# A graph network's forward pass on one core: sources of the 512-wide layer prepared one step earlier, and first-stage rows stored by another queue

## The chip, the cores and the metric

The kernel runs on one core of a Trainium2 chip. The metric is the device time of the whole program in microseconds. Each core has TensorE (PE), VectorE (DVE), ScalarE (ACT), GpSimd (POOL) and SyncE (SP); each runs its own queue of instructions in order, and they meet at semaphores.

## The reference

A graph of 6250 nodes and 100,000 edges, sorted by destination, with 256 values a node. Two residual blocks follow each other:

```
h = relu(layernorm(x)); x = x + attention_layer(h, edges)      # 8 heads, softmax over incoming edges, two batch norms
h = relu(layernorm(x)); x = x + gin(gin(gin(h)))
gin(h) = ((1 + eps) * h + segment_sum(h[src], dst)) @ w + b     # widths 256 -> 512 -> 512 -> 256, relu between
```

The first table stage of this text computes `layernorm`, `relu`, the three projections and the attention scores of every node. The 512-wide layer of this text is the segment sum over rows of 512 values, with the matrix `w3` (512 to 256) applied behind it.

## The kernel before

The nodes are cut into 50 blocks of 125. Phases follow each other with a barrier of all engines and a clearing of the semaphores between them: preparation of edges and of a block adjacency matrix, the first table stage, attention, dense layers, then three aggregation layers, of which `wide_layer` is the second.

**First table stage.** Two helpers matter. `place(b, j)` gives a block with its parity `s`, its index `i` of that parity, and its slot `t` of four x buffers. `over_steps(engine, stages)` writes an engine's program as steps; in step b it runs each `(stage, lag)` on block b - lag. SyncE loads x (`load_x`, L582), waiting from block 4 on for `norm_ready` of the block that had the buffer before. VectorE takes the moments of block b, normalises block b-1 and finishes block b-3 (`finish`: adds biases to the products, reduces to scores, fills `row[s]`, of which there are two). ScalarE takes square roots and copies the turned block; TensorE turns and projects. GpSimd stores `row[s]` to `table0` (`store_row`, L629), after one store of a spare row for each parity (`first_store`), which makes the count on `row_stored` start at one.

**The 512-wide layer.** For every block, GpSimd gathers the rows of the edges' sources from the table in device memory: a round is 17 indirect DMAs of 128 rows of 512 floats into the single buffer `gathered`, in four parts of 4, 4, 4 and 5 tiles; each part waits until TensorE has used that part of the round before (`quarters_used`). VectorE makes 17 one-hot matrices from the destinations, and TensorE adds one-hot times gathered rows in a PSUM bank (L2297, two instructions for each of the 17 products). Then follow `finish` on VectorE (adds the own row and the bias: L2178, L2181), `turn` and `down` on TensorE (the product with `w3_sb`, L2335), `store`, `keep_upper` on ScalarE and `halve` on VectorE, which split the result into an upper and a lower part for the next layer (L2189, L2191, L2216).

Four of the 50 blocks (43, 45, 47, 49: `tabled`) are not gathered. Their sums are made densely in four PSUM banks of their own: for each source block m, its 125 rows are split in an upper and a lower half (`split_source` on VectorE, L2166 and L2168, into the single buffer `source_cut` and half of `source[r]`), ScalarE casts the adjacency part and the upper half (`cast_source`, L2237 and L2239, then issues the load of source m+2), and TensorE multiplies (`source_sums`, L2317, eight products). `source`, `part` and `source_rows` have two buffers each; `source_used[r]` tells that TensorE is done with one.

This layer's `over_steps(engine, stages, beside, early)` runs the stages of step b and then `beside` for source b + `AHEAD`, with `AHEAD = 8` on all three engines. Sources 0 to `early` - 1 come before everything; then the stages of lag 0 for block 0, then the sources up to 7; step 0 has the source alone. Order on the engines in step b:

```
TensorE  rounds of b, turn of b-1, down of b-2, products of source b+8
ScalarE  copy_turned of b-1, store of b-2, keep_upper of b-5, cast of source b+8
VectorE  one-hots of b, finish of b-1, halve of b-4, split of source b+8
```

VectorE runs about a step in front of the others: it makes the one-hots of b+1 while TensorE multiplies block b.

Of the kernel before, what the change touches and what calls it, by code (L numbers as in the profile page):

```python
# [23 lines left out]
BLOCKS = N // NB  # L24
PAIRS = BLOCKS // 2
# [32 lines left out]
AHEAD = 8  # L58
# [34 lines left out]
def build(nc, x, src, dst, Wq, bq, Wk, bk, Wv, bv, Wo, bo, W1, b1, W2, b2, g1, be1, g2, be2,  # L93
# [12 lines left out]
    with ExitStack() as ctx:  # L106
# [63 lines left out]
        def first_store(engine, stored):  # L170

            n = next(spare_rows)
            engine.dma_start(spare[n:n + 1, :], identity[0:1, :]).then_inc(stored, 16)  # L173

        def block_rows(table, b):
            return table[bass.ds(b * NB, NB), :]
# [362 lines left out]
        with ExitStack() as phase:  # L539
# [37 lines left out]
            @block.sync  # L577
            def _(sp):
                def load_x(k):
                    if not isinstance(k.b, int) or k.b >= 4:  # L580
                        sp.wait_ge(norm_ready[k.s], k.i - 1)
                    sp.dma_start(x_sb[k.t][:, :], block_rows(x, k.b)).then_inc(x_loaded[k.t], 16)  # L582

                over_steps(sp, [(load_x, 0)])

            @block.vector
            def _(dve):
# [30 lines left out]
                    order.restart()  # L618

                over_steps(dve, [(statistics, 0), (normalise, 1), (finish, 3)])  # L620

            @block.gpsimd
            def _(pool):
                for s in range(2):
                    first_store(pool, row_stored[s])

                def store_row(k):
                    wait_apart(pool, row_ready[k.s], k.i + 2, 2)
                    pool.dma_start(block_rows(table0, k.b), row[k.s][:, :]).then_inc(row_stored[k.s], 16)  # L629

                over_steps(pool, [(store_row, 3)])
                for s in range(2):
                    pool.wait_ge(row_stored[s], 16 * (PAIRS + 1))

            @block.scalar
            def _(act):
# [1300 lines left out]
        def wide_layer(n, table, w):  # L1937
            k_tiles = w // P
            with ExitStack() as phase:
# [51 lines left out]
                def total_of(s, i):  # L1991
                    return tabled_ps[i - (PAIRS - TABLED)] if tabled(s, i) else sum_ps[s]

                def over_steps(engine, stages, beside=None, early=0):


                    def step(b, j=0):
                        for stage, lag in stages:
                            if b >= first_step and 0 <= b - lag < BLOCKS:
                                stage((b - lag) % 2, 2 * j + (b - lag) // 2)  # L2000
                        if beside is not None and b < BLOCKS - AHEAD:
                            beside(b % 2, b % 4, j + (b + AHEAD) // 4)

                    first_step = 0
                    if beside is not None:
                        for m in range(early):
                            beside(m % 2, m % 4, m // 4)
                        for stage, lag in stages:
                            if lag == 0:
                                stage(0, 0)  # L2010
                        for m in range(early, AHEAD):
                            beside(m % 2, m % 4, m // 4)
                        first_step = 1
                    for b in range(6):
                        step(b)
                    with engine.Fori(0, (BLOCKS - AHEAD - 10) // 4) as j:
                        for b in range(6, 10):
                            step(b, j)
                    for b in range(BLOCKS - AHEAD - 4, BLOCKS + 6):
                        step(b)  # L2020
# [96 lines left out]
                def _(dve):  # L2117
# [74 lines left out]
                                          upper[s][:, :], ALU.subtract).then_inc(lower_ready[s], 1)  # L2192
                        order.restart()

                    over_steps(dve, [(rounds_of, 0), (finish, 1), (halve, 4)], split_source, 6)

                @block.scalar
                def _(act):
# [55 lines left out]
                    for r in range(2):  # L2254
                        load_source(r, r)
                    load_parts(0)
                    over_steps(act, [(load_weights, 0), (copy_turned, 1), (store, 2), (keep_upper, 5)], cast_source, AHEAD)
                    for s in range(2):
                        act.wait_ge(stored[s], 16 * (PAIRS + 1))

# [108 lines left out]
```

## Time and profile before

| | |
|---|---|
| median of 3 runs | 4454.34 us (4452.92 to 4461.15) |
| the profiled execution: time, span | 4454.23 us, 4452.6 us |
| mean granted TensorE clock | 0.885 of 2.4 GHz |
| busy: PE, POOL, DVE, ACT | 80%, 57%, 48%, 28% of the span |
| first table stage | about 313 to 551 us |
| 512-wide layer | about 2742 to 3869 us |

The profile gives each group of instructions its busy time, its idle time before them, and what ended that idle time. A matmul of this kernel's floats is two instructions. The busy share is a mean over stages with different limits; it says little about either stage here.

### The profile page before, as it was taken

What the parts mean: (1) busy time and instruction counts of PE and PEld (TensorE: products, weight loads), DVE (VectorE), ACT (ScalarE), POOL (GpSimd) and SP (SyncE); (2) the same over time, 40 slices, a digit from 0 to 9 for tenths busy, and PEclk for the clock granted to TensorE, in tenths of its full rate; (3) what the DMA queues carried; (4) which work ended last, traced back from release to release, by engine and by line L of the source; (5) the groups of instructions that cost most, each with busy time, mean ns of one, the idle gap of its engine ahead of it and who ended that gap; (6) DMA issues with size and microseconds to landing.
All of it is one profiled execution on the core that took longest, in us unless ns stands there. A gap on an engine that the chain in (4) does not pass through costs nothing. (4 is left out here: it accounts for less than half of the span.)

```text
span 4452.6 us, 70250 instructions
## 1 busy us (share of the span) xinstructions
PE 3560.6 (80%) x16469; PEld 2364.4 (53%) x16470; DVE 2157.3 (48%) x7818; ACT 1265.9 (28%) x2537; POOL 2558.3 (57%) x2766
## 2 busy tenths in 40 slices
PE   3876557777777778876999997888888988788887
PEld 1223345555555557764777774444444444466665
DVE  6987667777777773362222221323322232233333
ACT  3972122222222222372333332001111011122222
POOL 5001177777777760035666663677776776477776
PEclk9999967787877789957999998999999999888888
DMA  4432144444444430067888885777777777599999
GB/s 141 173 155 59 49 112 111 112 112 112 112 112 112 112 101 1 29 188 211 244 245 245 244 243 166 223 233 232 235 235 231 234 234 227 181 286 294 296 293 268
DMA packets 388059, 801.61 MB, mean 180 GB/s; under 512 B 81225, under 2 KB 147513, under 8 KB 384614
## 3 DMA queue, kind: packets, MB, share of 16 engines
q0 software_dynamic: 244224, 577.30, 45.9%
q10 hardware_dynamic: 86354, 138.42, 9.7%
q1 hardware_dynamic: 57360, 84.55, 5.8%
q8 instruction: 44, 0.72, 0.1%
q14 instruction: 77, 0.62, 0.0%
HBM read 699.79 MB, written 100.24 MB: 180 GB/s over the span
## 5 line engine op out<-in xcount | busy, mean ns | idle before, releaser
L1702 POOL DMA_INDIRECT l_gathered<-table,record x850 | 809.5, 952 | 375.6 <-issue 245.8
L815 POOL DMA_INDIRECT a_gathered<-table,record x850 | 810.1, 953 | 302.9 <-issue 256.9
L2107 POOL DMA_INDIRECT l_gathered<-table,record x782 | 749.7, 959 | 374.2 <-issue 261.8
L2297 PE MATMUL bank<-l_gathered,l_onehot 128*125 128x512 f32 x1564 | 699.1, 605 | 18.7 <-DVE l_onehot L2152 15.6
L1139 PE MATMUL bank<-a_gathered,a_onehot 128*125 128x264 f32 x1700 | 520.3, 466 | 75.8 <-DVE a_gathered L943 75.7
L2297 PEld LDWEIGHTS bank<-l_gathered,l_onehot 128*125 128x125 f32 x1564 | 301.7, 194 | 397.5 <-issue 382.9
L1804 ACT ACTIVATE l_part<-l_packed 128x1000 fp32r<-128x1000 bf16 (+1 forms) x300 | 314.4, 1072 | 543.3 <-PE bank L1880 378.9
L1139 PEld LDWEIGHTS bank<-a_gathered,a_onehot 128*125 128x125 f32 x1700 | 374.5, 229 | 171.9 <-DVE a_gathered L943 50.8
L1880 PE MATMUL bank<-rows_last,l_part 125*125 125x512 f32 x1250 | 328.0, 426 | 25.1 <-ACT l_part L1804 18.0
L1880 PE MATMUL bank<-rows_first,l_part 125*125 125x512 f32 x1250 | 308.7, 406 | 29.7 <-ACT l_part L1804 29.7
L1899 PE MATMUL bank<-l_gathered,l_onehot 128*125 128x512 f32 x850 | 245.6, 437 | 105.6 <-DMA l_gathered<-table,record 105.4
L1880 PEld LDWEIGHTS bank<-rows_last,l_part 125*125 125x125 f32 x1250 | 253.3, 205 | 96.0 <-issue 31.8
L1880 PEld LDWEIGHTS bank<-rows_first,l_part 125*125 125x125 f32 x1250 | 234.4, 188 | 99.4 <-issue 40.4
L2178 DVE SCALAR_TENSOR_TENSOR l_z<-l_own,one_eps,bank 125x512 f32<-125x512 f32 x50 | 37.3, 747 | 506.7 <-PE bank L2305 498.5
L2206 ACT ACTIVATE l_zT<-bank 128x500 f32<-128x500 f32 x50 | 29.4, 587 | 862.3 <-PE bank L2326 862.3
L943 DVE TENSOR_TENSOR a_gathered<-a_gathered,bank 128x1024 f32<-128x1024 f32 x200 | 244.1, 1283 | 31.6 <-ACT bank L1082 31.6
L1899 PEld LDWEIGHTS bank<-l_gathered,l_onehot 128*125 128x125 f32 x850 | 165.9, 200 | 167.1 <-DMA l_gathered<-table,record 124.6
L2317 PE MATMUL bank<-l_source,l_part 125*125 125x512 f32 x400 | 139.3, 508 | 135.1 <-ACT l_source L2239 129.5
L173 POOL DMA_DIRECT2D spare<-identity x6 | 3.1, 537 | 420.8 <-POOLq L161 420.8
L533 PE MATMUL bank<-d_code_hot,d_low_hot 128*128 128x250 bf16 x625 | 205.9, 378 | 22.9 <-DVE d_code_hot L495 5.4
L510 ACT ACTIVATE d_stage<-bank 128x500 bf16<-128x500 f32 (+1 forms) x325 | 220.7, 726 | 9.3 <-PE bank L533 7.0
L1763 DVE SCALAR_TENSOR_TENSOR l_work<-rows_first,one_eps,bank 125x256 f32<-125x256 f32 x50 | 24.0, 481 | 402.7 <-PE bank L1907 402.7
(276 smaller groups left out, 5415.6 us busy)
## 6 DMA issues: line engine op xcount, KB each, us to landing
l_packed<-adjacency ACTq DMA_DIRECT2D x201, 250.0 KB, 5.1
adjacency<-d_stage SPq DMA_DIRECT2D x25, 1562.5 KB, 5.2
l_packed<-adjacency ACTq DMA_DIRECT2D x100, 281.2 KB, 5.9
l_gathered<-table,record POOLq DMA_INDIRECT x1632, 4.8
a_gathered<-table,record POOLq DMA_INDIRECT x850
table<-rows_first POOLq DMA_DIRECT2D x50, 250.0 KB
table<-l_work ACTq DMA_DIRECT2D x50, 250.0 KB
l_source_rows<-table ACTq DMA_DIRECT2D x50, 250.0 KB
```

The source lines that it names most:

```text
L510: act.activation(stage[d % 2][:, :, GD * g0:GD * g1].rearrange("p h (g n) -> p g h n", n=GD), banks[(d * NH + h) % 7][:, 0:(g1 - g0) * COD ...
L533: pe.matmul(banks[n % 7][:, (g - g0) * CODES:(g - g0 + 1) * CODES], low_hot[at % HOT][:, :], code_hot[at % HOT][:, :], start=True, stop=Tr ...
L815: pool.indirect_dma_start(out=gathered0[s][:, j * TW:(j + 1) * TW], out_offset=None, in_=table0, in_offset=bass.IndirectOffsetOnAxis(ap=re ...
L943: dve.tensor_tensor(values[:, j0:j1], values[:, j0:j1], factors[:, j0:j1, :].unsqueeze(3).broadcast_to([P, j1 - j0, HEADS, DH]), ALU.mult) ...
L1139: last = pe.matmul(acc_ps[s][0:NB, 0:TW], onehot[s][:, j, :], rows[:, j, :], start=(j == 0), stop=(j == T - 1), skip_group_check=True)
L1702: pool.indirect_dma_start(out=gathered[g][:, j, :], out_offset=None, in_=table, in_offset=bass.IndirectOffsetOnAxis(ap=record[k.t][:, j, 0 ...
L1804: act.activation(part[r][:, 0:h1 - h0, :].rearrange("p h n -> p (h n)"), packed[r][:, 0:h1 - h0, :].rearrange("p h n -> p (h n)"), ACT.Cop ...
L1880: last = pe.matmul(sum_ps[k.s][0:NB, :], part[r][0:NB, h - h0, :], rows_sb[:, h, :], start=(h == 0), stop=False, skip_group_check=True)
L1899: last = pe.matmul(total, onehot[k.t][:, j, :], gathered[g][:, j, :], start=False, stop=(j == T - 1), skip_group_check=True)
L2107: pool.indirect_dma_start(out=gathered[:, j * w:(j + 1) * w], out_offset=None, in_=table, in_offset=bass.IndirectOffsetOnAxis(ap=record[t] ...
L2297: last = pe.matmul(total[0:NB, 0:w], onehot[t][:, j, :], rows[:, j, :], start=False, stop=(j == T - 1), skip_group_check=True)
L2317: last = pe.matmul(tabled_ps[d][0:NB, 0:w], part[r][0:NB, d, :], source[r][:, half * w:(half + 1) * w], start=(first and half == 0), stop= ...
```

## The change

In the first table stage SyncE, not GpSimd, writes the stores of the rows, and x is loaded two blocks ahead of the step (lag -2), so that in a step of SyncE's program a load stands before a store. In the 512-wide layer, `over_steps` gets the distance as an argument; VectorE's split and ScalarE's cast use `AHEAD + 1`, while TensorE keeps `AHEAD`. In step b these two engines then prepare source b+9.

```diff
@@ -581,7 +581,18 @@
                         sp.wait_ge(norm_ready[k.s], k.i - 1)
                     sp.dma_start(x_sb[k.t][:, :], block_rows(x, k.b)).then_inc(x_loaded[k.t], 16)
 
-                over_steps(sp, [(load_x, 0)])
+                for s in range(2):
+                    first_store(sp, row_stored[s])
+
+                def store_row(k):
+                    wait_apart(sp, row_ready[k.s], k.i + 2, 2)
+                    sp.dma_start(block_rows(table0, k.b), row[k.s][:, :]).then_inc(row_stored[k.s], 16)
+
+                for b in range(2):
+                    load_x(place(b))
+                over_steps(sp, [(load_x, -2), (store_row, 3)])
+                for s in range(2):
+                    sp.wait_ge(row_stored[s], 16 * (PAIRS + 1))
 
             @block.vector
             def _(dve):
@@ -618,19 +629,6 @@
                     order.restart()
 
                 over_steps(dve, [(statistics, 0), (normalise, 1), (finish, 3)])
-
-            @block.gpsimd
-            def _(pool):
-                for s in range(2):
-                    first_store(pool, row_stored[s])
-
-                def store_row(k):
-                    wait_apart(pool, row_ready[k.s], k.i + 2, 2)
-                    pool.dma_start(block_rows(table0, k.b), row[k.s][:, :]).then_inc(row_stored[k.s], 16)
-
-                over_steps(pool, [(store_row, 3)])
-                for s in range(2):
-                    pool.wait_ge(row_stored[s], 16 * (PAIRS + 1))
 
             @block.scalar
             def _(act):
@@ -1991,15 +1989,16 @@
                 def total_of(s, i):
                     return tabled_ps[i - (PAIRS - TABLED)] if tabled(s, i) else sum_ps[s]
 
-                def over_steps(engine, stages, beside=None, early=0):
+                def over_steps(engine, stages, beside=None, early=0, ahead=AHEAD):
 
 
                     def step(b, j=0):
                         for stage, lag in stages:
                             if b >= first_step and 0 <= b - lag < BLOCKS:
                                 stage((b - lag) % 2, 2 * j + (b - lag) // 2)
-                        if beside is not None and b < BLOCKS - AHEAD:
-                            beside(b % 2, b % 4, j + (b + AHEAD) // 4)
+                        m = b + ahead
+                        if beside is not None and m < BLOCKS:
+                            beside(m % 2, m % 4, j + m // 4)
 
                     first_step = 0
                     if beside is not None:
@@ -2008,7 +2007,7 @@
                         for stage, lag in stages:
                             if lag == 0:
                                 stage(0, 0)
-                        for m in range(early, AHEAD):
+                        for m in range(early, ahead):
                             beside(m % 2, m % 4, m // 4)
                         first_step = 1
                     for b in range(6):
@@ -2192,7 +2191,7 @@
                                           upper[s][:, :], ALU.subtract).then_inc(lower_ready[s], 1)
                         order.restart()
 
-                    over_steps(dve, [(rounds_of, 0), (finish, 1), (halve, 4)], split_source, 6)
+                    over_steps(dve, [(rounds_of, 0), (finish, 1), (halve, 4)], split_source, 6, AHEAD + 1)
 
                 @block.scalar
                 def _(act):
@@ -2254,7 +2253,7 @@
                     for r in range(2):
                         load_source(r, r)
                     load_parts(0)
-                    over_steps(act, [(load_weights, 0), (copy_turned, 1), (store, 2), (keep_upper, 5)], cast_source, AHEAD)
+                    over_steps(act, [(load_weights, 0), (copy_turned, 1), (store, 2), (keep_upper, 5)], cast_source, AHEAD, AHEAD + 1)
                     for s in range(2):
                         act.wait_ge(stored[s], 16 * (PAIRS + 1))
 
```

## Rows read from the trace of the kernel before

**Rows 1.** Groups by line, 2740 to 3860 us: busy us, mean ns | idle before, releasers.
```profile
L2107 POOL DMA_INDIRECT l_gathered<-table,record x782 | 749.7, 959 | 374.2 <-issue 261.8 <-PE bank L2297 112.4
...
L2317 PE MATMUL bank<-l_source,l_part 125*125 125x512 f32 x400 | 139.3, 508 | 135.1 <-ACT l_source L2239 129.5 <-DVEq L2169 5.6
...
L2168 DVE TENSOR_TENSOR l_source<-l_source_rows,l_source_cut 125x512 fp32r<-125x512 f32 x50 | 34.6, 692 | 7.5 <-DVE l_source_cut L2166 4.1
L2181 DVE TENSOR_TENSOR l_z<-l_z,l_c_sb 125x512 f32<-125x512 f32 x50 | 34.6, 692 | 7.4 <-DVE l_z L2178 3.5
...
L2191 DVE TENSOR_TENSOR rows_last<-l_result,l_upper 125x256 f32 (+1 forms) x50 | 21.3, 427 | 12.0 <-DVE l_upper L2189 11.4
```

**Rows 2.** Window: length, busy PE, PEld, DVE, ACT, POOL, PEclk, DMA share, GB/s.
```profile
2948.30:3755.39 807.09, 714.53 (x1966) 370.06 (x1965) 239.87 (x829) 84.47 (x175) 569.34 (x597) 0.95 0.77 234
```

**Rows 3.** Timeline of one step: start, length, instruction, idle before and releaser.
```profile
3333.18 0.61 ACT L2239 ACTIVATE l_source<-l_source_cut 125x512 fp32r<-125x512 f32 x1
...
3333.94 3.38 PE L2317 MATMUL bank<-l_source,l_part 125*125 125x512 f32 x8 [2.57 <-ACT l_source L2239]
...
3337.53 14.88 PE L2297 MATMUL bank<-l_gathered,l_onehot 128*125 128x512 f32 x34
...
3342.05 0.94 POOL L2107 DMA_INDIRECT l_gathered<-table,record  x1 [2.15 <-PE bank L2297]
```

**Rows 4.** Windows: a whole step, the stretch after its wait, an early step.
```profile
3328.98:3352.25 23.27, 20.70 (x57) 10.96 (x56) 6.99 (x24) 2.41 (x5) 16.25 (x18) 0.93 0.78 248
3334.00:3337.50 3.50, 3.50 (x9) 2.59 (x10) 1.35 (x3) 0.00 (x0) 2.73 (x3) 0.55 0.82 260
2847.70:2868.60 20.90, 19.31 (x57) 9.78 (x56) 6.22 (x22) 2.00 (x4) 15.72 (x18) 1.00 0.81 236
```

**Rows 5.** Timeline of POOL: first gathers of rounds, and one long gather (2913.28).
```profile
2817.89 1.03 POOL L2107 DMA_INDIRECT l_gathered<-table,record  x1 [4.78 <-PE bank L2297]
...
2904.53 0.95 POOL L2107 DMA_INDIRECT l_gathered<-table,record  x1 [0.30 <-PE bank L2297]
...
2913.28 1.43 POOL L2107 DMA_INDIRECT l_gathered<-table,record  x1 [0.30 <-issue]
...
2926.76 0.95 POOL L2107 DMA_INDIRECT l_gathered<-table,record  x1 [0.30 <-issue]
...
2950.10 0.94 POOL L2107 DMA_INDIRECT l_gathered<-table,record  x1 [2.10 <-PE bank L2297]
...
3732.27 0.95 POOL L2107 DMA_INDIRECT l_gathered<-table,record  x1 [0.95 <-PE bank L2297]
```

**Rows 6.** Timeline: the last gather of a round, and TensorE's products on it.
```profile
2925.51 0.95 POOL L2107 DMA_INDIRECT l_gathered<-table,record  x1 [0.30 <-issue]
...
2932.67 4.56 PE L2297 MATMUL bank<-l_gathered,l_onehot 128*125 128x512 f32 x10 [1.59 <-DMA l_gathered<-table,record]
```

**Rows 7.** Timeline of the wide layer's start.
```profile
2804.54 0.48 DVE L2166 TENSOR_SCALAR l_source_cut<-l_source_rows 125x512 int32<-125x512 int32 x1 [14.32 <-PE bank L2317]
...
2811.72 16.55 PE L2297 MATMUL bank<-l_gathered,l_onehot 128*125 128x512 f32 x34 [3.38 <-DVE l_onehot L2152]
```

**Rows 8.** First stage (groups, SyncE's wait, timeline), and a first-store pair elsewhere.
```profile
L629 POOL DMA_DIRECT2D table<-row x50 | 26.6, 531 | 201.6 <-DVEq L617 201.6
...
SPq L582 <- DVEq L604: 176.0, 46, 6.7
...
313.45 21.26 SPq L582 DMA_DIRECT2D x_sb<-in_x  x9
...
316.62 0.43 DVE L594 BATCH_NORM_STATS2 six<-x_sb 125x6 f32<-125x256 f32 x1 [10.64 <-DMA x_sb<-in_x]
...
419.76 0.69 DVE L610 TENSOR_TENSOR qk<-bank,bqkv_sb 125x512 f32<-125x512 f32 x1 [0.32 <-DVE norm L602]
...
424.13 0.69 DVE L610 TENSOR_TENSOR qk<-bank,bqkv_sb 125x512 f32<-125x512 f32 x1 [0.24 <-DVE norm L602]
...
2742.14 0.64 ACTq L173 DMA_DIRECT2D spare<-identity  x2
```

## The prediction

> **What bounds the kernel now.** I read the page first, then windows by stage, to find the two stages that the diff touches: the first table stage (about 313 to 551 us) and the 512-wide layer (about 2742 to 3869 us). The groups by line of the wide layer [rows 1] name two idle times. TensorE sits idle 135.1 us before the source products of L2317, nearly all of it until ScalarE's cast (L2239). GpSimd sits idle 374.2 us before its gathers, but 261.8 us of that is the 0.30 us that separates any two gathers, plus the stage's start; 112.4 us is waiting for TensorE's products of L2297, because there is one `gathered` buffer. The window over the steady part [rows 2] shows TensorE busy 714.5 of 807.1 us at a mean granted clock of 0.95. Neither engine is saturated, so the step must be read as a loop.
>
> One step of that loop is in [rows 3]. TensorE's product with `w3_sb` ends at 3331.37 (3333.94 - 2.57), ScalarE works through its copies and casts in order, and its cast at 3333.18 releases the source products at 3333.94: 2.57 us of idle. TensorE then works without a pause through the next round. GpSimd has finished its 17 gathers and waits 2.15 us for the first four tiles of that round; 1.85 us of this is beyond its usual 0.30. So the step closes on TensorE: 23.27 us, 20.70 busy and 2.57 waiting [rows 4]. The second window of that group shows what the wait costs besides: right behind it the granted clock is 0.55 of full, that is 1.2 GHz for most of 3.5 us. An early step of the same work, before `keep_upper` joins ScalarE's queue, waits only 1.59 us (20.90 - 19.31), keeps 2.4 GHz, and is busy for 19.31 us. The lowered clock costs 20.70 - 19.31 = 1.39 us a step.
>
> **What the wide-layer edit removes.** After it, ScalarE in step b casts source b+9 and TensorE multiplies source b+8, whose cast is a step old. `source` and `part` have two buffers each, so the cast of b+9 needs only the products of b+7, done a step earlier. The 2.57 us go, and their 1.39 us with them: TensorE could step in 19.31 us.
>
> **Where the stall goes.** GpSimd cannot follow. By the mean gather of 959 ns [rows 1] and 0.30 between them, a round of 17 takes 21.40 us. The trace has a stretch in which GpSimd was the bound: six rounds from 2817.89 to 2950.10, less the last wait beyond 0.30 (2.10 - 0.30 = 1.80) [rows 5], are 130.41 us or 21.74 each. The longest is 2904.53 to 2926.76, 22.23 us; the last is 2926.76 to 2948.30, 21.54 us, and in it TensorE idled for landing rows [rows 6], which is the state I expect to last. I take 21.65, between 21.54 and 21.74; the ends are 21.40 and 22.23. TensorE's idle reappears as 21.65 - 19.31 = 2.3 us before the last tiles of a round.
>
> Can one buffer sustain that? The chain through two rounds is: 17 gathers, 21.4; landing of the last, 2926.46 to 2932.67 = 6.2 [rows 6]; ten products, 4.3; the rest of TensorE's step, 19.31 less 34 products of 0.43 = 4.7; eight products of the next round, 3.5; and the release, from about 3341.0 (3337.53 plus 3.5) to 3342.05, 1.05 [rows 3]. That is 41.2 for two rounds, 20.6 each, under 21.65. Two lowered clocks in it (2.8) make 22.0 each.
>
> **Other waits of the edit.** VectorE's split of b+10 now needs the products of b+8 in the same stretch of time. Those follow the `w3_sb` product at once and end about 2 us later (3.38 us less the 1.39 that the lowered clock costs), while the split anyway waits for ScalarE's cast, which ends at 3333.79 [rows 3]. Cost nothing. Queued behind the split are the one-hots for a round TensorE begins a whole round later, some 15 us of cover; without it each 1 us late would cost 1 us. The loads of source rows and of `packed` move with the casts on ScalarE's queue; each keeps one step of lead.
>
> The ramp has no such cover. TensorE waits 3.38 us for the one-hots of block 1, which stand behind the split released at 2804.54 [rows 7]. One more split now stands between: 0.48 plus 0.69 for its two operations [rows 1, 7] and about 0.4 of waits, so 1.6 us once. Bounds 0 (absorbed) and 3.4 (as much again as the idle).
>
> **Sum for the wide layer.** Between the round at 2950.10 and the one at 3732.27 [rows 5] lie 34 rounds in 782.17 us, 23.00 each. Saved: 34 x (23.00 - 21.65) = 46.1; plus 1.8, the wait before 2950.10; less 1.6 for the ramp: 46.3 us. The tail (blocks 43 to 49) has no source products; it starts earlier by this much and keeps its length.
>
> **First table stage.** VectorE is the bound: its `qk` additions are 4.37 us apart [rows 8], and the store's 0.53 us on GpSimd, after 201.6 us of waiting, is on nobody's path. SyncE also waits, 176.0 us in 46 times, for `norm_ready`. Now load b+2 stands behind the store of b-4, which waits for VectorE's `finish` of that block, in the same VectorE step as the normalisation it waited for before. It is issued up to some 3 us later and needed two steps (8.7 us) later, against 3.2 us from issue to use (313.45 to 316.62 [rows 8]). A row buffer is reused two steps on, too. Steady cost nothing; without that cover it would be the lateness times 50. At the start two stores of a spare row go ahead of the first x load on SyncE: ScalarE's queue took 0.64 us for such a pair [rows 8], so +0.6. The last store's landing by SyncE isn't in the trace: 0 either way, within 1 us, since the store through GpSimd took 0.53 us of issue.
>
> **A rule weighed.** A gather of 1.43 us begins at 2913.28 [rows 5], beside VectorE's `l_z` addition with two SBUF inputs (L2181); most take 0.94. The Trainium skill, "SBUF — State Buffer", section "Who interferes with whom", says that such a VectorE instruction contends with a GpSimd instruction that reads SBUF and that the second to issue blocks. By full blocking a round would be 23.0 (rival B, whose price is from rows), by the stretch it is 21.74; the trace agrees in kind, less in size.
>
> **Total.** The profiled execution is 4454.23 us (span 4452.6), 0.1 below the median of 4454.34. 4454.23 - 46.3 + 0.6 = 4408.5; I say 4408. Each 0.1 us of round length is 3.4 us.
>
> **Rivals.**
> A. The clock falls anyway. TensorE's new 2.3 us of idle is near the 2.57 that lowered it, and the two-round chain then gives 22.0; with gathers lengthened as in the longest round, about 22.3. For: the size of the idle. Against: 1.59 us left the clock whole, and the new idle may split into parts. Time: 4408 + 34 x 0.65 = 4430. Chance 0.13.
> B. Gathers lengthen. If L2168, L2181 and L2191 (0.69, 0.69, 0.43) [rows 1] each held one up in full, a round is 17 x 1.245 + 1.81 = 22.98: the saving vanishes, 4454. The same result if the casts stay late because ScalarE waits for the cut. Against: the mean gather is 0.959. Chance 0.05.
> C. Slower, by the first stage: store and load in one queue make x late. From the point at which issue to use exceeds 8.7 us, VectorE's step grows; to outweigh 46 us it must be 0.94 us a block longer, so 9.7 us from issue to use, three times the 3.2 shown. Say 1.2 us a block: 4408 + 60 = 4468. Chance 0.03.
> D. Gathers stay at 21.40 or better: 4408 - 8.5 = 4400 or just under; 0.10, within the range.
> The forecast itself, 21.50 to 22.0 a round (4403 to 4420), has 0.69.
>
> **Numbers.** Likeliest 4408. The range runs from 4398 (21.40, and 2 us from an easier ramp) to 4430 (rival A, above 22.23's 4428). It leaves out B, C, the slower half of A and the edge of D, about 0.17. Changes of 0.2% (8.9 us) are about what a measurement of this kernel tells from none: faster 0.91 (forecast, A, D, less a little), same 0.05 (B), slower 0.04 (C and what I overlooked).
>
> **What would show it.** In the profile of the changed kernel the idle before L2317 falls from 135.1 to under 40 us, what is left being the ramp. GpSimd's waits for L2297 shrink to the first ones; TensorE gains "DMA l_gathered" idle of some 60 to 80 us. A round's first gathers are 21.5 to 22.0 apart; the wide layer is some 46 us shorter. In the first stage L610 stays 4.37 apart on average of plain steps. The forecast is wrong if gathers lengthen past 1.05 us on average, if the granted clock stays at 0.95 with a new wait in its place, or if `six` (L594) waits for `x_sb` beyond the start.

## The result, and the profile after

The changed kernel takes 4399.88 us (median of 4 runs, 4392.37 to 4403.69) against 4455.59 (4 runs): a ratio of 0.9871, interval 0.9854 to 0.9888. Forecast were 4408 and 4398 to 4430. The profiled execution took 4402.32 us (span 4400.7), 51.9 less than that of before.

I read the two stages first, by windows: the first table stage, the wide layer, and the layer's 34 steady rounds. The columns are as in [rows 2].

```profile
312.72:547.13 234.41, 154.22 (x500) 81.18 (x500) 164.74 (x500) 51.39 (x201) 0.00 (x0) 0.98 0.19 56
...
2738.51:3814.87 1076.36, 934.90 (x2668) 475.06 (x2668) 337.78 (x1136) 121.24 (x250) 759.62 (x786) 0.96 0.77 235
2944.72:3680.51 735.79, 666.10 (x1905) 336.41 (x1904) 237.91 (x816) 82.15 (x170) 559.68 (x579) 0.99 0.81 248
```

The wide layer was 1126.66 us long (2742.14 to 3868.80, from its first store to that of the next layer) and is now 1076.36: 50.3 less. Its 34 steady rounds went from 782.17 us [rows 5] to 735.79, 21.64 each, at a clock of 0.99 in place of 0.95 [rows 2]. The first stage went from 237.14 us (313.45 to 550.59) to 234.41: 2.7 less. What lies before, between and behind these two stages differs by 0.2 to 2.0 us each and is together 1.1 us longer.

The same groups by line as in [rows 1], in the changed kernel (the lines are one lower):

```profile
L2106 POOL DMA_INDIRECT l_gathered<-table,record x782 | 756.1, 967 | 317.3 <-issue 268.0 <-PE bank L2296 49.3
...
L2296 PE MATMUL bank<-l_gathered,l_onehot 128*125 128x512 f32 x1564 | 717.7, 611 | 101.0 <-DMA l_gathered<-table,record 83.6 <-DVE l_onehot L2151 17.1
...
L2316 PE MATMUL bank<-l_source,l_part 125*125 125x512 f32 x400 | 112.2, 426 | 32.8 <-ACT l_source L2238 27.9 <-DVEq L2168 4.9
```

TensorE's idle time before the source products fell from 135.1 to 32.8 us, and their mean from 508 to 426 ns, which is the clock. New are 83.6 us in which TensorE waits for gathered rows. GpSimd's waits for TensorE's products fell from 112.4 to 49.3. The bound has moved to another engine, and the timeline of TensorE shows one round of it:

```profile
3296.86 6.25 PE L2296 MATMUL bank<-l_gathered,l_onehot 128*125 128x512 f32 x10 [1.88 <-DMA l_gathered<-table,record]
...
3303.44 1.89 PE L2334 MATMUL bank<-l_w_sb,l_zT 128*125 128x256 f32 x8
3304.98 2.21 PE L2316 MATMUL bank<-l_source,l_part 125*125 125x512 f32 x8
3307.02 0.38 PE L2289 MATMUL bank<-zeros 128*125 128x512 bf16 x1
3307.24 10.46 PE L2296 MATMUL bank<-l_gathered,l_onehot 128*125 128x512 f32 x24
3318.33 4.56 PE L2296 MATMUL bank<-l_gathered,l_onehot 128*125 128x512 f32 x10 [0.63 <-DMA l_gathered<-table,record]
```

The source products stand directly behind L2334, without the 2.57 us of [rows 3], and take 2.21 us in place of 3.38; the idle time now lies before the last rows of a round.

### The profile page after: what moved, and what is told of

Same layout as the page of the kernel before. It is cut to its first block and busy times, and to the rows that moved or that the text cites. A ratio compares the mean times of both kernels' runs of the same rounds, so it can differ in the third digit from the quotient of the medians.

```text
span 4400.7 us, 70234 instructions
## 1 busy us (share of the span) xinstructions
PE 3535.3 (80%) x16469; PEld 2343.3 (53%) x16470; DVE 2158.5 (49%) x7818; ACT 1265.7 (29%) x2537; POOL 2536.4 (58%) x2714
## 5 line engine op out<-in xcount | busy, mean ns | idle before, releaser
L2296 PE MATMUL bank<-l_gathered,l_onehot 128*125 128x512 f32 x1564 | 717.7, 611 | 101.0 <-DMA l_gathered<-table,record 83.6
L1897 PE MATMUL bank<-l_gathered,l_onehot 128*125 128x512 f32 x850 | 249.5, 443 | 109.0 <-DMA l_gathered<-table,record 108.9
L495 DVE TENSOR_SCALAR d_code_hot<-d_code_iota,d_lists 128x250 bf16<-128x250 bf16 x625 | 187.9, 302 | 0.0
L1926 PE MATMUL bank<-l_w_sb,l_work 128*125 128x512 f32 x400 | 179.8, 593 | 0.0
```

What stands on the lines that cost most here:

```text
L495: dve.tensor_scalar(code_hot[g % HOT][:, :], code_iota[:, :], lists[:, c, 1, k:k + 1], None, ALU.is_equal).then_inc(pair_ready, 1)
L1897: last = pe.matmul(total, onehot[k.t][:, j, :], gathered[g][:, j, :], start=False, stop=(j == T - 1), skip_group_check=True)
L2296: last = pe.matmul(total[0:NB, 0:w], onehot[t][:, j, :], rows[:, j, :], start=False, stop=(j == T - 1), skip_group_check=True)
```

## Experiments

Two kinds of chip are in these runs. The result above and the experiments e5 to e8 and e12 come from chips on which the kernel before takes 4455 to 4458 us ("usual" below). On two others it took 6269 us (e1 to e4) and 6275 us (e9 to e11). There, comparisons hold only among one chip's own runs, and I use them for what their own traces show.

**The parts of the change, on another chip (e1 to e4).** The wide-layer edit alone; the first-stage edit alone; and the full change with only one of the two engines one step ahead:

```
 e3: over_steps(dve, ..., split_source, 6, AHEAD + 1)   # VectorE ahead
     over_steps(act, ..., cast_source, AHEAD)           # ScalarE as before
 e4: over_steps(dve, ..., split_source, 6)              # VectorE as before
     over_steps(act, ..., cast_source, AHEAD, AHEAD + 1)  # ScalarE ahead
```

> Only the edit of the 512-wide layer (split and cast one step ahead); the first table stage as before. Theory: the wide layer is the seat of the gain, TensorE's wait for the cast is gone and GpSimd's gathers set a step of 21.6 us; the layer takes 1076 to 1077 us against 1126.7 before, and the whole 50 us less than before (about 4405). Rival: the first stage's edit carries a share worth more than its own 3 us by moving what follows; then this kernel gains under 45 us.

> Only the edit of the first table stage; the wide layer as before. My prediction had +0.6 us. The two traces show 2.7 us less for this stage, all of it between the last VectorE instruction of the stage and the first of the next (8.5 us before, 4.2 us after). Theory: this exit follows the queue that stores; it is 4.2 us here as well, and the whole is 2 to 4 us faster, too little for the clock on the wall but plain in the trace. Rival: the exit is scatter of one execution; then it is 8 us here.

> The changed kernel with ScalarE's cast back at 8 steps and only VectorE's split at 9. VectorE's split of a source then waits in the same step for ScalarE's cast of the one before it, because source_cut is one buffer, and the one-hots of the next block are queued behind that split. Theory: TensorE waits for one-hots each step, the step is near 26 us, and the time is 4520 to 4600, slower than before. Rival: the one-hots have the 15 us of cover that I claimed for them; then it is like before, about 4455.

> The changed kernel with VectorE's split back at 8 steps and only ScalarE's cast at 9. VectorE runs a step in front of TensorE, so the cut that ScalarE's cast needs comes about 1 us later than the cast would begin, and the cast is still a step old when TensorE wants it. Theory: ScalarE's distance alone carries the gain, 4400 within 5. Rival: ScalarE stands at the cut so long that its later copies hold TensorE up; then 4420 or more.

Measured: before 6269.47; wide layer alone 5896.63, ratio 0.9411 (0.9384 to 0.9439); first stage alone 6259.53, 0.9982 (0.9964 to 1.0); ScalarE's cast as before 6407.32 (one run); ScalarE's cast ahead and VectorE's split as before 5855.91 (one run). The times expected for the parts of the wide layer were all wrong, for the wait of L2317 for the cast is here not 2.6 us but about 14. The exit of the first stage expected for the first-stage edit, 4.2 us, was right. By sign the times order the parts: with the cast one step ahead there is the gain, with the split alone ahead there is none. That the latter comes out slower goes with VectorE's wait for the cast in that trace (the first fence below, over its wide layer). The cast alone ahead, with 5855.91 us, is no slower than the wide-layer edit, so what the split's step adds isn't shown. No part of the change was run alone on a usual chip; there the two edits are told apart by their stages alone.

The same two edits once more (e10, e11), again on such a chip:

> The wide-layer edit alone, on a chip on which the kernel before takes its usual 4455 us. Theory (the two edits add): 50 us less than before from the layer and nothing from the first stage, 4403 to 4406; the exit of the first table stage stays at 8.51 us. Rival (the first stage's saving of 2.7 us is not real): 4400, equal to the changed kernel.

> The first-stage edit alone, on a chip on which the kernel before takes its usual 4455 us. Theory: 2.7 us less than before (4.3 from the exit of the stage, less 0.6 at its start and 1 inside), 4452 to 4453, a ratio of 0.9994. Rival: no difference or some us more, as x stands behind stores in SyncE's queue, 4455 to 4460. A difference this small may lie within the interval; the stage's length in the profile (237.1 us before, 234.4 after) then decides.

Measured: before 6275.15; wide layer alone 5930.44, 0.946 (0.9431 to 0.949); first stage alone 6241.39, 0.9963 (0.994 to 0.9986). The absolute times expected can't be judged. Waits of the wide layer with the split alone ahead, then the timelines of ScalarE and TensorE in one step, first-stage edit alone (wide layer as before) and wide-layer edit alone:

```profile
DVE l_source_cut L2165 <- ACT l_source L2238: 656.8, 25, 30.5
```

```profile
4328.12 0.38 ACT L2210 ACTIVATE l_result<-bank 125x256 f32<-125x256 f32 x1 [12.41 <-DMA pair_records<-arena]
...
4330.76 3.75 PE L2315 MATMUL bank<-l_source,l_part 125*125 125x512 f32 x8 [13.95 <-ACT l_source L2237]
```

```profile
4317.07 0.38 ACT L2213 ACTIVATE l_result<-bank 125x256 f32<-125x256 f32 x1 [6.44 <-DMA pair_records<-arena]
...
4311.39 2.21 PE L2318 MATMUL bank<-l_source,l_part 125*125 125x512 f32 x8
```

ScalarE stands still for 12.41 us ahead of a copy that waits 1.14 us in the kernel before on the usual chip; the transfer named had landed long ago, so the profile doesn't show the cause. With the old order TensorE waits behind it, 13.95 us. With the new one its source products start at 4311.39 while ScalarE is still stalled, since their cast is a step old. So the edit is worth 5 to 6% there, where the whole change is worth 1.3% here.

What carries over is the exit of the first stage, which these stalls don't touch. From VectorE's last operation to the next stage's first, it is 8.50 and 8.51 us in the runs of the wide-layer edit alone, where GpSimd stores the rows, and 4.21 and 4.24 us in those of the first-stage edit alone. In the changed kernel, on the usual chip:

```profile
312.72 0.54 SPq L173 DMA_DIRECT2D spare<-identity  x2
...
313.31 1.42 SPq L582 DMA_DIRECT2D x_sb<-in_x  x4
...
542.50 0.42 DVE L627 TENSOR_TENSOR row<-bank,bqkv_sb 125x256 f32<-125x256 f32 x1
547.13 0.06 DVE L827 MEMSET a_scanned<- 8x1 f32 x1 [4.21 <-PEq L161]
```

and in the kernel before:

```profile
541.66 0.42 DVE L616 TENSOR_TENSOR row<-bank,bqkv_sb 125x256 f32<-125x256 f32 x1
550.59 0.06 DVE L829 MEMSET a_scanned<- 8x1 f32 x1 [8.51 <-PEq L161]
```

What fills the exit is in both traces too. GpSimd and SyncE each wait for the landing of their last store and then execute a DRAIN, an instruction of the engine's sequencer at the end of a stage (L539), before the barrier. By `--source L539`, in the kernel before and then in the changed one (duration in ns, start in us):

```profile
L539 POOLq DRAIN  x1: 4302/4302/4302, 545.1 to 545.1; - x1
...
L539 SPq DRAIN  x1: 7/7/7, 546.0 to 546.0; - x1
...
L539 POOLq DRAIN  x1: 46/46/46, 312.7 to 312.7; - x1
```

The landing is waited for until 544.9 in the kernel before and until 545.8 in the changed one, 2.9 us after VectorE's last operation in both. What differs is the DRAIN: 4.30 us on GpSimd when it has issued the stage's 52 stores, 0.05 us and at the stage's start when it has issued none, 0.01 us on SyncE. It is the same 4.30 us in all six traces in which GpSimd stores these rows, and it is the whole gain of the exit.

The two stores at the stage's start delay the first load of x by 0.6 us (312.72 to 313.31), and the exit gives 4.3 back. With the 2.7 us that the stage is shorter, 1.0 us more was spent inside it, all of it while the stage starts up: the first addition into `qk` comes 1.3 us later after the stage's start than before (13.24 in place of 11.97 us), and the 49 steps that follow take 0.3 us longer (214.74 in place of 214.45).

**Who bounds a round? (e5, e6)** Half of the source products left out, in the changed kernel and in the kernel before. The second half of `source` holds the lower-order parts of the split rows, so it is those that are not summed (the expectation calls the halves columns, wrongly).

```
                             for d in range(TABLED):
-                                for half in range(2):
+                                for half in range(1):
```

> The changed kernel with four of the eight products of a source left out (only the first 256... columns' half of source rows, half 0 of two, is summed: the result differs). TensorE loses 4 x 0.42 to 0.49 us, 1.7 to 2.0 us, of the 19.6 us that it is busy in a round of the wide layer. Theory (GpSimd's gathers now bound a round): the 34 rounds stay 21.6 us apart, within 0.1, and the time within 5 us of the changed kernel's (4395 to 4405). Rival (TensorE still bounds a round): the rounds come down by 1.7 to 2.0 us, to about 19.8, and the layer by 58 to 68 us (4335 to 4342).

> The kernel before with the same four of eight products of a source left out (the result differs). Theory: in the kernel before TensorE's chain (its busy time and the wait for ScalarE's cast, 2.6 us) sets 23.00 us a round, so 1.7 to 2.0 us less of it are gained until the gathers bind at 21.6: rounds of 21.6 us at best, 21.0 if TensorE alone bound, so 21.6 to 21.8, and 40 to 47 us off the time (4408 to 4416). Rival (the wait for the cast, which starts from the start of the previous round, grows by what the products lose): rounds stay 22.8 to 23.0 and the time within 8 us of before.

Measured, one run each: 4397.02 and 4478.82 us, beside 4455.36 for the kernel before. The 34 rounds of the changed kernel with 136 products fewer, by windows:

```profile
2939.43:3674.14 734.71, 641.36 (x1769) 312.12 (x1768) 237.52 (x816) 82.14 (x170) 558.63 (x578) 0.98 0.81 249
```

TensorE is busy for 24.7 us less and the rounds take 21.61 in place of 21.64: TensorE isn't the bound any more, as the theory said. In the kernel before, neither theory nor rival held: with less work it took 23 us longer. Groups, timeline and windows of that kernel, over its 34 rounds (2948.22 to 3756.80, 23.78 each) and in one step:

```profile
L2297 PE MATMUL bank<-l_gathered,l_onehot 128*125 128x512 f32 x1158 | 552.6, 639 | 0.0
...
L2317 PE MATMUL bank<-l_source,l_part 125*125 125x512 f32 x136 | 46.1, 468 | 88.7 <-ACT l_source L2239 88.7
...
L2290 PE MATMUL bank<-zeros 128*125 128x512 bf16 x34 | 21.1, 620 | 32.7 <-issue 32.7
```

```profile
3346.65 1.16 PE L2317 MATMUL bank<-l_source,l_part 125*125 125x512 f32 x4 [2.58 <-ACT l_source L2239]
3348.76 0.68 PE L2290 MATMUL bank<-zeros 128*125 128x512 bf16 x1 [0.95 <-issue]
3349.24 17.53 PE L2297 MATMUL bank<-l_gathered,l_onehot 128*125 128x512 f32 x34
```

```profile
2948.22:3756.80 808.58, 687.21 (x1770) 332.15 (x1769) 236.44 (x816) 82.06 (x170) 552.07 (x578) 0.91 0.74 227
...
3349.24:3354.24 5.00, 5.00 (x7) 2.01 (x7) 3.71 (x18) 0.00 (x0) 2.75 (x3) 0.50 1.01 355
```

The wait for the cast is as long as ever, 2.6 us a step; the cast doesn't depend on these products. But where eight products stood there are four, and 0.96 us of "issue" follow them (32.7 over 34), of which the kernel before has 0.04 (1.5 us in its 34 rounds). In the changed kernel with the same four products there is none: its TensorE hasn't just waited. So this idle time belongs to the wait as well; what TensorE does in it the profile doesn't show. After the two idle times the clock is 0.50 for at least another 5.0 us, now under the 34 gathered products, which take 17.53 us in place of 14.88 [rows 3].

The 34 rounds of the kernel before, for comparison:

```profile
L2297 PE MATMUL bank<-l_gathered,l_onehot 128*125 128x512 f32 x1158 | 513.0, 602 | 0.0
L2317 PE MATMUL bank<-l_source,l_part 125*125 125x512 f32 x272 | 97.1, 516 | 88.6 <-ACT l_source L2239 88.6
...
L2290 PE MATMUL bank<-zeros 128*125 128x512 bf16 x34 | 18.3, 539 | 1.5 <-issue 1.3
...
2950.10:3732.27 782.17, 692.03 (x1906) 358.26 (x1905) 236.02 (x816) 82.05 (x170) 552.38 (x578) 0.95 0.77 234
```

Over these rounds the source products take 51.0 us less (46.1 in place of 97.1), but the gathered ones 39.6 more (552.6 in place of 513.0), so that TensorE is busy for 687.2 us in place of 692.0. The clock has taken back nearly all that the removed work gave, and the 31.2 us of new "issue" idle make the rounds longer, 26.4 us in all.

**Is it the wait, or the clock behind it? (e9, e12)** The last result suggests that the clock could be bought back with useless work. So: ten products of zeros, added with value zero, ahead of the wait in the kernel before, with the cast as late as it was.

```
+                        if not first:
+                            for fill in range(10):
+                                pe.matmul(tabled_ps[0][0:NB, 0:w], zeros[:, 0:NB], zeros[:, 0:w],
+                                          start=False, stop=False, skip_group_check=True)
                         pe.wait_ge(part_cast[r], v + 1)
```

> The kernel before with ten products of zeros (128x512 bf16, added with value zero to a running sum, some 0.21 us each at 2.4 GHz) put on TensorE's queue just ahead of its wait for ScalarE's cast, so that TensorE is busy in most of the 2.57 us of that wait. Nothing else changes: the cast is as late as before. Theory (the wait's second price is the lowered clock behind it, 1.39 us a step, and in the kernel with half of the products it was the longer idle that cost more by the clock): the clock stays near 1.0, a step comes down from 23.0 to 21.65 (23.0 less 1.39 is 21.6, and there the gathers bind), and the time by 40 to 47 us, to 4408 to 4415, with useless work added and the wait still there. Rival (the clock falls for other reasons, or products of zeros do not keep it): steps of 23.0 or, where the fillers end later than the cast, a few tenths more, 4450 to 4475.

> The kernel before with the ten products of zeros ahead of the wait for ScalarE's cast, once more, for a chip on which that wait is 2.57 us as in the kernel before's trace (on the last one it was some 14 us, the fillers took 2.3 of it and 10.2 us stayed, with the lowered clock behind it). Theory (the clock is the wait's second price): 0.3 us of idle stays, the granted clock is near 1.0, a step is 21.6 to 21.7 and the time 4408 to 4415. Rival (the clock falls for other reasons, or products of zeros do not keep it): steps of 23.0 to 23.3 and 4450 to 4475. If the wait is again over 10 us, the run tells nothing of this.

On the other chip it told nothing (6286.11 against 6275.15: 10.2 us of the wait stayed). On the usual one: 4434.28 us against 4458.33, ratio 0.9942 (0.9925 to 0.9959). Its 34 rounds by windows, its groups, and TensorE in one step:

```profile
2956.36:3715.18 758.82, 733.16 (x2246) 379.26 (x2245) 237.38 (x817) 82.07 (x170) 552.23 (x578) 1.00 0.78 242
```

```profile
L2321 PE MATMUL bank<-l_source,l_part 125*125 125x512 f32 x272 | 71.2, 403 | 15.3 <-ACT l_source L2239 15.3
...
L2290 PE MATMUL bank<-zeros 128*125 128x512 bf16 x34 | 14.1, 414 | 10.4 <-issue 10.2
```

```profile
3349.35 2.32 PE L2314 MATMUL bank<-zeros 128*125 128x512 bf16 x10
3352.19 2.10 PE L2321 MATMUL bank<-l_source,l_part 125*125 125x512 f32 x8 [0.52 <-ACT l_source L2239]
3355.08 0.42 PE L2290 MATMUL bank<-zeros 128*125 128x512 bf16 x1 [0.79 <-issue]
```

The clock is 1.00 throughout, and a round takes 22.32 us, 0.69 less than before, with ten useless products more and the cast no earlier. So the lowered clock is a price of its own: the theory's mechanism holds. Its size was too large. Without the fillers' 78.9 us TensorE is busy for 654.3 us in place of 692.0, so the clock is worth 1.11 us a round, not 1.39. Of this 0.42 are given back: fillers and the wait that is left take 94.2 us in place of the 88.6 of waiting (0.16 a round), and the "issue" idle grows from 1.5 to 10.4 us (0.26). The change itself gets the clock and the wait, 1.36 us a round.

**The bias by TensorE (e8).** If gathers bind, what lengthens a gather should show. VectorE's addition of the bias (L2180) was taken away; TensorE adds it as identity times bias rows in place of the product of zeros. ScalarE loads weights and bias ahead of the layer's steps for it.

```
-                            pe.matmul(total[0:NB, 0:w], zeros[:, 0:NB], zeros[:, 0:w], start=True, stop=True)
+                            pe.matmul(total[0:NB, 0:w], identity[0:NB, 0:NB], c2_sb[:, :], start=True, stop=False, ...)
...
-                        order.step(dve.tensor_tensor(z[s][:, :], z[s][:, :], c2_sb[:, :], ALU.add))
```

> The changed kernel, with the bias of the wide layer put into the sums by TensorE (identity times the bias rows as first product, in place of the product of zeros) and VectorE's addition of the bias taken away, 0.7 us a round. Theory (GpSimd's gathers bound a round, and those beside that addition take 1.144 in place of 0.948 us): 0.15 us a round and 5 us in the 34 rounds less, 6 to 7 us in the layer, so 4393 to 4395; TensorE's first product grows by 0.5 us at most and has 3 us a round to spare. Rival 1 (the gather is long there for another reason, or other operations lengthen it as much): rounds stay at 21.64, time within 1.5 us of the changed kernel. Rival 2 (TensorE is closer to the bound than thought): 0.3 to 0.5 us a round slower, 10 to 17 us more.

Measured: 4395.01 us (4391.23 to 4400.43), ratio to before 0.9865 (0.9848 to 0.9881). Its interval covers that of the changed kernel (0.9854 to 0.9888), so by time it is a draw. By the profile the rounds are 21.56 us (733.02 for 34), 2.8 us less in all, between theory and rival 1: the gathers take 4.1 us less (555.58 in place of 559.68, against 5 expected), and one pause of 1.6 us between two of them gives 1.3 back. TensorE's longer first product cost nothing: it was busy 680.18 of the 733.02 us.

**The store edit in another stage (e7).** The same edit in the stage that makes `x` and `table` for the mixed layers: its two stores a block moved from GpSimd's queue to SyncE's, loads two blocks ahead.

```
-            @block.gpsimd    # store_x1 and store_rows
+                over_steps(sp, [(load_x, -2), (store_x1, 1), (store_rows, 6)])
```

> The changed kernel, with the stores of the dense stage between the first stage and the mixed layers (two a block) moved from GpSimd's to SyncE's queue as the change did in the first stage, its x loads two blocks ahead. Theory (a stage whose last stores GpSimd issues leaves 4.3 us later than one with SyncE's): 3 to 5 us faster than the changed kernel, 4395 to 4397. Rival 1 (the 4.3 us came from something else in the first stage): within 1 us of the changed kernel. Rival 2 (a load of x stands in SyncE's queue behind a store that waits for its block's late steps): the stage's step grows, 0.3 us or more a block, 15 us and more slower than the changed kernel.

Measured: 4457.59 us, ratio to before 1.0006 (0.9996 to 1.0016), so 58 us slower than the changed kernel. That is the time of rival 2, and by more than its 15 us, but not its mechanism. The stage by windows, in the changed kernel and then in this one, and SyncE's queue in a step of this one:

```profile
1868.00:2007.34 139.34, 96.89 (x400) 83.56 (x400) 93.48 (x306) 97.80 (x301) 53.72 (x102) 0.54 0.65 178
```

```profile
1868.00:2066.76 198.76, 97.28 (x400) 84.90 (x400) 96.76 (x306) 97.63 (x301) 0.00 (x0) 0.53 0.33 121
```

```profile
1948.55 0.94 SPq L1416 DMA_DIRECT2D table<-rows_first  x1
1949.78 1.33 SPq L1404 DMA_DIRECT2D g_x_sb<-in_x  x1
1951.42 0.77 SPq L1411 DMA_DIRECT2D x<-g_x_sb  x1
1952.77 1.02 SPq L1416 DMA_DIRECT2D table<-rows_first  x1
```

Hardly any engine works longer (VectorE by 3.3 us), yet the stage grows by 59.4 us, 1.2 a block. A block needs three DMAs from one queue, and here one follows another in 1.2 to 1.6 us: 4.2 us for this block (1948.55 to 1952.77), 4.0 on average, against 2.8 in the changed kernel (139.34 over 50). It isn't a store that waits for a late step: SyncE waits for other engines 15 us in all, in 14 times. By `--dma`, the changed kernel, then this one:

```profile
DMA packets 15758, 24.83 MB, mean 178 GB/s; under 512 B 2053, under 2 KB 8353, under 8 KB 15754
...
DMA packets 18608, 23.97 MB, mean 121 GB/s; under 512 B 715, under 2 KB 13114, under 8 KB 18604
```

With both queues 178 GB/s are moved, with SyncE's alone 121, at 122 to 126 in nearly every slice of the stage. After SyncE's last issue, which ends at 2070.2, the queue goes on moving rows at this rate until about 2080. So what the one queue moved was the bound: 500 KB a block at 124 GB/s are 4.1 us. In the first stage a block has two DMAs of 125 and 129 KB and takes 4.4 us; the queue moves 56 GB/s there.

The theory's own claim, that this stage's exit gets 4.3 us shorter, failed as well. From VectorE's last operation to ScalarE's first DMA of the next stage it is 14.32 us in the changed kernel (2007.34 to 2021.66) and 14.92 here (2066.76 to 2081.68). GpSimd's DRAIN of 8.55 us, behind 104 stores, is gone; but SyncE waits for the landing of its last stores until 2080.5, 10.3 us after it issued the last.

Not run: GpSimd's stores ending early in a stage, which would tell whether its DRAIN can be hidden.

## Why the prediction was right

- **What bounds the kernel now; what the edit removes.** Right, with both terms. The wait went (135.1 to 32.8 us, under 40 as forecast), and the clock with it (0.95 to 0.99). The fillers show that the two are separate: the clock alone was worth 1.11 us a round. The 1.39 of the prediction was read off one step of 23.27 us, which was longer than the mean of 23.00; it isn't in the sum, since the gathers bind first.
- **Where the stall goes.** Right: 21.65 us a round were forecast and 21.64 measured; 46.1 us for 34 rounds, and 46.4 measured. That it fits to 0.01 is luck, as the choice was between 21.54 and 21.74. The half products confirm the bound: 21.61 without half of TensorE's source work. By parts it is 17 gathers of 0.968 us and 17 gaps of 0.305. TensorE's new idle time is 83.6 us, a little above the 60 to 80 forecast.
- **The two-round chain and rival A.** The clock did fall in some rounds: in the one before the round shown, idle times of 0.71 and 1.88 us stood close together, and behind them the clock was 0.73 and ten products took 6.25 us in place of 4.56. The mean of 0.99 says how seldom. Rival A at 22.3 us did not come.
- **The start and the tail of the layer.** TensorE's wait for the one-hots of block 1 grew as forecast, from 3.38 to 5.14 us (1.8, where 1.6 were forecast), but TensorE came to it 1.4 us earlier, for a reason not shown. So the start (to round 8) was 1.75 us shorter, where -1.8 and +1.6 make 0.2. The tail, forecast unchanged, was 2.2 us shorter. The prediction took it to hold no source products, but one group of them still stood behind 3732.27, with its wait of 2.42 us and its 3.65 us of work at the low clock; it now takes 2.21 us and waits for nothing. With the rounds these are the 50.3 us, against 46.3.
- **The first stage.** Nothing was lost in the steady steps, as forecast. The exit, "0 either way, within 1 us", is the term that was mis-sized: -4.3 us. The issue time of a store (0.53 us) was taken for what GpSimd's stores cost at the end of a stage, where its DRAIN takes 4.30. The start was 0.6 us as forecast by the stores of spare rows, and 1.0 more.
- **The rule weighed, and rival B.** The mean gather of the steady rounds went from 0.956 to 0.968 us; B needed 1.05. But the rule was read wrongly, see below.
- **Rivals C and D.** No load in the first stage was late beyond the start. C's outcome is real in a shorter step: in the stage of 2.8 us a block it cost 59 us, by what one queue could move. D's 21.40 us a round would need gathers of 0.954.

Altogether 46.4 + 1.75 + 2.2 + 2.7 = 53.0 us less, of which about 1 us is given back in the other stages: 51.9. Against the profiled time the forecast of 4408.5 missed by 6.2 us: 4.0 by the layer, nearly all of it in the start and the tail, and 3.3 by the first stage, less the 1.1 given back. The median lies 2.4 below the profiled time, and so only 1.9 us inside the range's lower end of 4398; single runs fell below it. The range held by a small margin, and partly by luck: its lower end was built from faster gathers and an easier ramp, while what made the kernel faster than 4408 was the exit, the tail and the start.

## What to carry to other kernels

A wait in front of TensorE has two prices, its length and the clock behind it, and both must be read before less or more work is put there. Removing it is worth no more than the distance to the next bound: here 23.00 to 21.64 us, though TensorE is busy for only 19.6 of these. When DMAs are gathered on one queue, compare what the queue must move in a step with what it moved at its fullest, and not only the issue times. At a stage's end look at the exit too: the landing of the last stores, and GpSimd's DRAIN.

## What the runs showed of the hardware

**A gather that starts inside a two-input operation of VectorE is held up by most of it.** In the changed kernel's 34 rounds, 24 gathers had begun before an addition of the bias (L2180, 0.69 us) that ran beside them and took 0.946 us; 28 began during one and took 1.122 on average, the longer, the earlier in it they began:

```profile
3345.90 0.69 DVE L2180 TENSOR_TENSOR l_z<-l_z,l_c_sb 125x512 f32<-125x512 f32 x1
3345.95 1.46 POOL L2106 DMA_INDIRECT l_gathered<-table,record  x1 [0.30 <-issue]
```

One that began 0.05 us into it took 1.46, 0.22 into it 1.28 to 1.30, 0.41 into it 1.10, from 0.58 on 0.95: each ends as if it had begun 0.56 us after the addition did. VectorE's subtraction in the split (L2167), also with two inputs in SBUF, does the same: begun 0.26 us into it, a gather took 1.25. The Trainium skill, "SBUF — State Buffer", section "Who interferes with whom", says that issue order decides which of the two is blocked. The trace agrees for the gather that comes second, with up to 0.51 of the addition's 0.69 us as the price. For the addition that comes second it doesn't: beside the 24 gathers that had begun before, it took its 0.69 us as ever. The prediction read the rule as an average and found it "less in size". For a gather it is most of the operation, but rare. In the kernel before, none of the 34 additions was met (all 34 gathers beside one had begun earlier), but the subtraction (L2168 there) was met in 33 of 34 rounds, 0.43 to 0.64 us into it, and those gathers took 1.04 us on average. GpSimd's restarts hung on TensorE's products there and so came at much the same place of every step; once the gathers run freely they drift across VectorE's work.

**GpSimd's stores have a price at the end of a stage.** The exit of the first stage was 8.50 to 8.51 us in the six traces with GpSimd's stores, and 4.20 to 4.25 in the eight with SyncE's. The difference is GpSimd's DRAIN ahead of the barrier: 4.30 us behind 52 stores. In the other stage it was 8.55 us behind 104 stores, so 0.08 us a store in both, and 0.03 where GpSimd had stored nothing (e7). What the engine does in it the profile doesn't show.

**One queue can be the bound.** SyncE's queue, with rows of 1 and 2 KB, moved 122 to 126 GB/s all through a stage in which it was behind (e7); GpSimd's and SyncE's together moved 178 in the same stage.

**The same kernel on two other chips** took 41% longer, with single engines standing still for 6 to 14 us at a time in the steps shown and nothing in the profile to account for it. What it is stays open. One step of slack between ScalarE and TensorE hid most of it in the wide layer: 25.0 us a round (850.76 for 34), against 34.3 (1166.71) with the wide layer as before (e10 and e11).
